# Second-block weights centred by a matmul and split bank by bank inside the first block's attention

## The reference

```
block 0, per batch:  h = film(rmsnorm(x)); Q, K, V = h @ q_w, h @ k_w, h @ v_w  (one head, 128 wide)
                     x = x + softmax(Q K^T / sqrt(128)) V @ proj_w
                     x = x + gelu(film(rmsnorm(x)) @ mlp_w1) @ mlp_w2           (128 -> 512 -> 128)
block 1, per batch:  h = layernorm(x) + shift(cond);  q, k, v = h @ Wqkv.T      (16 heads of 64)
                     q, k = layernorm of each head's 64 values
                     x = x + concat(softmax(q k^T / 8) v) @ Wout.T
experts:             8 experts each take the 128 tokens of highest gate, a gelu MLP each, added back
```

## Time and profile before

| | before |
|---|---|
| median of 3 runs | 473.82 us (473.6 to 474.19) |
| the profiled execution | 473.62 us, its span 471.9 us |
| mean granted TensorE clock | 0.949 |
| PE busy | 419.6 us (89% of the span) |
| DVE / ACT / POOL busy | 303.2 / 299.7 / 186.6 us |
| chain that ended last | PE 72%, DVE 5% |

### The profile page before, as it was taken

The page is one execution under the profiler, slowest core; times in us unless marked ns, Lnnn a source line. Parts: engine busy times, 40 slices in busy tenths (PEclk is TensorE's granted clock), DMA queues, the critical chain, the costliest instruction groups (busy, mean ns, idle before and its releaser), DMA issues.

```text
span 471.9 us, 8986 instructions
## 1 busy us (share of the span) xinstructions
PE 419.6 (89%) x2918; PEld 363.0 (77%) x2918; DVE 303.2 (64%) x761; ACT 299.7 (64%) x675; POOL 186.6 (40%) x148
## 2 busy tenths in 40 slices
PE   2998965389999999999999999999998987639996
PEld 1577554269989999999999998999997886528794
DVE  3574365556776776776777677677676437985233
ACT  3255523357878878878887887887886666305631
POOL 5102472734543553553454454355354004235000
PEclk9999997579999999999999999999999997858999
DMA  8300000650000000000000000000000000000001
GB/s 230 106 1 1 1 0 0 193 209 1 1 3 1 1 1 0 0 0 0 0 0 0 0 0 0 0 0 0 0 0 2 1 0 2 0 2 0 1 1 44
DMA packets 7492, 9.49 MB, mean 20 GB/s; under 512 B 371, under 2 KB 4270, under 8 KB 7470
## 3 DMA queue, kind: packets, MB, share of 16 engines
q1 hardware_dynamic: 5646, 7.11, 4.9%
q10 hardware_dynamic: 1824, 2.10, 1.6%
HBM read 8.68 MB, written 0.52 MB: 20 GB/s over the span
## 4 chain that ended last, share of the span: by engine, by line
PE 72%; DVE 5%; issue 1%; ACT 1%; DVEq 0%
PE bank L1255 24%; PE bank L1040 16%; PE pair L1221 9%; PE pair L1240 6%; PE pair L1239 6%; PE bank L1406 2%; PE pair L1040 1%; PE pair L1327 1%; DVE at_least L941 1%; PE pair L1362 1%; PE bank L1362 1%; PE pair L1398 1%; PE pair L1417 1%; PE pair L1379 1%; PE bank L1398 1%
## 5 line engine op out<-in xcount | busy, mean ns | idle before, releaser
L1255 PE MATMUL bank<-v_s,probs_T 128*128 128x128 f32 x1024 | 135.4, 275 | 2.7 <-ACT probs_T L596 1.9
L857 DVE TENSOR_REDUCE negmax<-pair 128x1 f32<-128x512 f32 x128 | 88.1, 688 | 74.8 <-PE pair L1240 74.8
L1255 PEld LDWEIGHTS bank<-v_s,probs_T 128*128 128x128 f32 x1024 | 126.5, 192 | 5.9 <-issue 2.5
L416 POOL TENSOR_TENSOR qk_rstd<-qk_ms,minus_half 128x8 f32<-128x8 f32 x32 | 55.1, 1721 | 132.2 <-DVE qk_ms L828 132.0
L596 ACT ACTIVATE probs_T<-bank 128x512 f32<-128x512 f32 x128 | 76.6, 598 | 44.6 <-PE bank L1040 44.6
L590 ACT ACTIVATE probs<-pair,negmax 128x512 f32<-128x512 f32 x128 | 88.2, 689 | 15.9 <-DVE negmax L857 15.8
L1040 PE MATMUL bank<-ident,probs 128*128 128x128 f32 x512 | 76.6, 272 | 0.0
L1040 PEld LDWEIGHTS bank<-ident,probs 128*128 128x128 f32 x512 | 62.7, 140 | 13.2
L1239 PE MATMUL pair<-k_s,q_s 128*128 128x512 f32 x128 | 61.4, 480 | 0.4 <-ACT probs L590 0.4
L1240 PE MATMUL pair<-k_low,q_s 128*128 128x512 f32 x128 | 50.8, 397 | 0.0
L426 POOL TENSOR_TENSOR q_s<-kq,k_s 64x512 fp32r<-64x512 f32 x32 | 44.0, 1376 | 13.5 <-DVE k_s L843 8.7
(11 more groups left out here) (260 smaller groups left out, 659.5 us busy)
## 6 DMA issues: line engine op xcount, KB each, us to landing
fc_raw<-in_L_cond_fc2s_dram SPq DMA_DIRECT2D x1, 2048.0 KB, 15.2
x_in<-in_x_dram ACTq DMA_DIRECT2D x1, 512.0 KB, 4.7
w<-in_L_cond_mlp_w_dram SPq DMA_DIRECT2D x2, 256.0 KB, 3.2
wout<-in_L_cond_Wout_dram SPq DMA_DIRECT2D x1, 512.0 KB
b_all<-in_L_cond_b2s_dram SPq DMA_DIRECT2D x1, 512.0 KB, 11.5
out_dram<-final SPq DMA_DIRECT2D x2, 256.0 KB, 2.4
film<-in_L_cond_film_w_dram SPq DMA_DIRECT2D x2, 128.0 KB, 5.1
wq<-in_L_cond_q_w_dram SPq DMA_DIRECT2D x1, 64.0 KB, 7.3
```

The costliest lines, as they stand in the source:

```text
L416: pool.tensor_tensor(qk_rstd[:, :, :].rearrange("p c t -> p (c t)"), qk_ms[:, :, :].rearrange("p c t -> p (c t)"), minus_half[:, 0:2 * NC] ...
L857: dve.tensor_reduce(negmax[:, s:s + 1], bank[s % 2][:, :], AX, ALU.max, negate=True)\
L1255: last = pe.matmul(bank[4][:, c * D:c * D + D], probs_T[:, c % 2, k, :], v_s[:, slot, k, :], start=(k == 0), stop=(k == NC - 1))
```

## The change

- `w_all` and `wmean` go. A constant matrix `centring` (identity minus 1/64 in the two 64x64 diagonal blocks) is built on POOL at the start. The four banks of q and k weights are products raw x `centring` (L1151 of the changed file) where they were transposes: they come out turned and centred.
- Each bank is split at once: ACT rounds it from PSUM into `w_hi`, DVE subtracts, PSUM minus `w_hi`, into `w_lo` (`weights_low`, L768). POOL has no part in it any more.
- The six first banks are made in iterations g = 1 to 6 of block 0's attention, all in PSUM bank 7, so each waits until the one before is copied and split; in DVE's list the subtraction of bank g-2 stands behind the maximum and the scaling of iteration g. Of the other four, one stands before `proj0(1)`, one after, two after the up products of batch 0.
- The MLP goes batch by batch: up products 0 to 3, transposes of batch 1's norm, two weight banks, `down0(0)`, up products 4 to 7, transposes of batch 0's second-block norm, `down0(1)`. POOL adds the MLP bias per batch. ACT writes batch 0's `h_T` in two halves and DVE splits it in two halves.
- `project(3)` moves into the first unit, behind the second chunk's scores, and ACT's and DVE's work on it with it. The first pieces and batch 1's norm are interleaved in another order.

```diff
             turned0(TC - 2)
...
+            act.wait_ge(mid_ready, 1)
+            square(x_mid, 0)
             turned0(TC - 1)
+            act.wait_ge(exp0_done, TC)
+            act.activation(table_call[:, 0:1], minus_half[:, 0:1], ACT.Gelu)
+            copy_weights(QK_BANKS + WOUT_BANKS)
             into_h(1)
+            act.wait_ge(mid_ready, 2)
+            square(x_mid, 1)
+            copy_weights(QK_BANKS + WOUT_BANKS + 1)
...
+            for n in range(HC):
+                gelu0(n)
+            for n in range(QK_BANKS + WOUT_BANKS + 2, W_BANKS):
+                copy_weights(n)
+            act.wait_ge(wT_done, W_BANKS + 1)
+            act.activation(wgate_T[:, :], bank[6][:, 0:E], ACT.Copy).then_inc(wT_copied, 1)
+            for n in range(HC, 2 * HC):
+                gelu0(n)
             act.wait_ge(norm_in, 1)
             square(xn, 0)
...
+            def weights_low(n):
+
+                dve.wait_ge(wT_copied, n + 1)
+                dve.tensor_tensor(weight_part(w_lo, n), weight_psum(n), weight_part(w_hi, n).bitcast(F32),
+                                  ALU.subtract).then_inc(w_split, 1)
+
             for g in range(TC + 1):
...
+                if 2 <= g <= QK_BANKS + 1:
+                    weights_low(g - 2)
...
+            for b in range(B):
+                at = slice(b * NC, b * NC + NC)
+                pool.wait_ge(norm_done, 3 + b)
+                pool.tensor_tensor(x_mid[:, at, :], x_mid[:, at, :],
+                                   mb0[:, :].unsqueeze(1).to_broadcast([P, NC, D]), ALU.add).then_inc(xmb_ready, 1)
...
+        def weight_bank(n):
+
+            return bank[7] if n < QK_BANKS + WOUT_BANKS else bank[5 + n % 2]
...
+            def make_weights(n):
+                dst = weight_bank(n)
+                if n == 0:
+                    pe.wait_ge(wqkv_in, 16)
+                    pe.wait_ge(v0_ready, 1)
+                    pe.wait_ge(centring_ready, 1)
+                elif n <= QK_BANKS + WOUT_BANKS:
+                    pe.wait_ge(wT_copied, n)
+                    pe.wait_ge(w_split, min(n, QK_BANKS))
+                if n < QK_BANKS:
+                    for c in range(4):
+                        last = pe.matmul(dst[:, c * P:c * P + P], wqkv_raw[:, 4 * n + c, :], centring[:, :],
+                                         start=True, stop=True)
...
             for g in range(TC + 3):
...
+                if 1 <= g <= QK_BANKS + WOUT_BANKS:
+                    make_weights(g - 1)
                 if g == NC + 3:
+                    pe.wait_ge(wT_copied, QK_BANKS + WOUT_BANKS)
                     proj0(0)
+            make_weights(QK_BANKS + WOUT_BANKS)
             proj0(1)
...
+            turn_norm(1, 0)
+            pe.wait_ge(mlp_in, 32)
+            pe.wait_ge(h_act, 2)
+            for n in range(HC):
+                up0(n)
+            turn_norm(1, 1)
+            for n in range(QK_BANKS + WOUT_BANKS + 2, W_BANKS):
+                make_weights(n)
+            down0(0)
...
+            for n in range(HC, 2 * HC):
                 up0(n)
+            turn_norm(2, 0)
             down0(1)
-            turn_norm(2, 0)
...
             project(0, 0, 0)
+            pe.wait_ge(h_split, 2)
             project(1, 1, 0)
+            pe.wait_ge(norm_in, 2)
+            turn_piece(0, 0)
             turn_norm(2, 1)
-            turn_piece(0, 0)
             turn_piece(1, 1)
-            pe.wait_ge(h_split, 2)
+            pe.wait_ge(h_split, 3)
             project(2, 2, 0)
-            project(3, 3, 0)
             body(0, first=True)
```

More of the change, by code:

```diff
@@ L543, in _ @@
                                bias=col("mlp_b1", c)).then_inc(gelu0_done, 1)
[L544 to L548 removed]
+            for n in range(HC):
[6 more added lines that the diff above has]
+                gelu0(n)
             act.wait_ge(norm_in, 1)
             square(xn, 0)
[L552 removed]
+            act.wait_ge(norm_T, 5)
+            for half in range(2):
+                act.activation(h_T[:, half * (N // 2):(half + 1) * (N // 2)],
+                               bank[1][:, half * (N // 2):(half + 1) * (N // 2)], ACT.Identity,
+                               bias=affine[:, 2, 1, 0:1], scale=affine[:, 2, 0, 0:1]).then_inc(h_act, 1)
             act.activation(table_call[:, 0:1], minus_half[:, 0:1], ACT.Exp)
[L554 to L556 removed]
             def piece_in(p, p_in):
@@ L601, in body @@
                     u = i * PER + j
+                    start = first and j == 0
                     for c in range(NC):
                         g = u * NC + c
-                        if c == 0 and not (last and j >= PER - 3):
+                        if c == (2 if start else 0) and not (last and j >= PER - 3):
                             piece_in(u + 3, j + 3)
@@ L607, in body @@
                             piece_affine(u + 2)
-                        if not (first and j == 0 and c < 2):
+                        if not (start and c < 2):
                             copy_probs(g - 2, c)
@@ L615, in _ @@
             piece_in(1, 1)
+            act.wait_ge(norm_in, 2)
+            square(xn, 1)
             piece_affine(0)
@@ L812, in _ @@
             sum_squares(2, 0)
-            rest = slice(POOL_HEADS, H)
-            dve.wait_ge(w_centred, 2)
-            dve.tensor_tensor(w_lo[:, rest, :], w_all[:, rest, :], w_hi[:, rest, :].bitcast(F32),
-                              ALU.subtract).then_inc(w_split, 1)
             scaled(2, 0, xn)
+            for half in range(2):
+                dve.wait_ge(h_act, 3 + half)
+                split_h(half * (N // 2), (half + 1) * (N // 2))
             block_out(1)
-            split_h(0)
-            sum_squares(2, 1)
             def piece_ss(p):
@@ L875, in body @@
                     u = i * PER + j
+                    start = first and j == 0
                     for c in range(NC):
                         g = u * NC + c
-                        if c == 3 and not (first and j == 0):
+                        if c == 3 and not start:
                             unit_out(u - 1, (j + 1) % 2, (j + 3) // 2 % 2)
                         chunk_max(g, c)
-                        if c == 0 and not (last and j >= PER - 3):
+                        if c == (2 if start else 0) and not (last and j >= PER - 3):
                             piece_ss(u + 3)
@@ L884, in body @@
                             piece_high(u + 2, j + 2)
-                        if c == 2 and not (last and j >= PER - 3):
+                        if c == (3 if start else 2) and not (last and j >= PER - 3):
                             piece_norm(u + 3, j + 3)
@@ L1264, in body @@
                         scores(g, u, c, j)
+                        if first and j == 0 and c == 1:
+                            project(3, 3, 0)
                         if c == 0 and not (last and j >= PER - 2):
```

191 lines of the change are left out of this document (74 added, 117 removed).

## The result

The changed kernel takes 478.84 us (median of 4 runs, 477.9 to 479.57) against 474.0 for the kernel before on the same chip: ratio 1.0105, 95% interval 1.0089 to 1.0122. The forecast was 478.7. The profiled execution took 478.36 us, its span 476.6, against 473.62 and 471.9 before.

A forecast was written before the change was run, and what follows sets the result against it. Before the loop at 105.33 the kernel was taken as bound in turn by full PE in attention, then PE's waits for DVE, POOL and ACT. Terms -0.2, +3.3 and +1.8 (clock) gave +5.1 on 473.62: 478.7 us; range 474.5 to 483.5.

The forecast's parts named there:

- two of its own signs: Before and in the loop: project(2) starts near 90, project(4) 3 to 5 us later than 103.83.
- Attention: Block 0's attention: chunks take 4.02 us instead of 2.19, banks waiting for DVE's split; ends at 47.25, not 39.90: +7.35.
- rival 2: Block 0's attention: the wait hides and a bank costs only its products; 3.7 us less, 475.0; chance 0.08.
- To the first up product: After block 0's attention: six banks of transposes and copies gone; up product at 52.0, before 46.92; 2.3 us won back.
- Batch 0's MLP: Block 0, up products through batch 0's down products: 62.6, before 61.2, a smaller POOL stall included; 3.6 us won back.
- Batch 0's second norm: After batch 0's last up products: transposes at 70.4, before 71.40, -1.0 in all.
- Down products of batch 1: Behind batch 0's second-norm transposes: first projection at 74.55 instead of 74.71, -0.2; plus +1.8 for half clock.
- Rival 1: Half clock takes all of down0(1), and the later DVE multiply waits for both POOL passes: 480.6 to 482.1; chance 0.23.
- First pieces: Before the loop: project(2) at 90.3, before 86.1, +4.2; piece 2's norm ready at 97.2 instead of 95.5, +1.7.
- Project(3) in the loop: Transposes and scores stand ahead: its first square at 101.8 instead of 98.51, loop start +3.3; this step +1.6.
- rival 4: Project(3) in the loop frees nothing, already in the sum; if PE did get ahead, 1.6 less: 477.1.
- Rival 3: Before the loop: clock stays full from 70 through project(3), making the kernel faster: 472.3 us; chance 0.1.

The follow-up runs named there:

- experiment 1: Changed kernel with the six weight banks of block 0's attention taking PSUM banks 7 and 6 in turn, not 7 alone: 475.38 us.
- experiment 2: Changed kernel with POOL's MLP bias of batch 0 issued ahead of its scale for batch 1's norm: 478.33 us.
- Experiment 5: Changed kernel with four dummy products of 512 columns ahead of the transposes of batch 0's second norm: 477.34 us.
- experiment 4: Changed kernel with project(3), and ACT's and DVE's work on it, back ahead of the unit loop: 478.89 us.
- experiment 8: Changed kernel with two POOL waits, so its subtractions of pieces 0 and 1 start only after DVE's norm multiply and h_lo: 478.6 us.
- experiment 9: Changed kernel with the four dummy products of experiment 5 plus short ones in PE's gaps up to the loop, leaving the one ahead of project(4): 474.97 us.
- 10: The kernel of experiment 7 with short dummy products in its gaps ahead of the loop, nine of them behind the wait they should fill: 470.95 us.
- experiment 12: The kernel of experiment 9 with ten more short dummy products in the wait ahead of project(4): 473.76 us.
- experiment 3: Changed kernel with batch 1's down products put back ahead of the transposes of batch 0's second norm: 476.29 us.
- 6: Changed kernel with the edits of experiments 1, 2 and 3 together: 471.82 us.
- 7: The kernel of experiment 6 with batch 1's second norm and split ahead of the first pieces' own work on ACT, DVE, POOL and PE: 470.04 us.
- 11: The kernel of experiment 10 with the nine dummy products moved ahead of their wait and ten more ahead of project(4): 466.72 us.

## Why the prediction was right

The sum (+5.1) and the time (478.7) hold, but not every term, and two of its own signs didn't come: project(2) near 90 (93.88), and project(4) 3 to 5 us later than 103.83 (5.73). In the old trace's time:

*Attention*, +7.35: measured 39.90 to 47.25, exact. The step behind it, a bank that waits for DVE's split, is shown by experiment 1; rival 2 (the wait hides) is out, since the period is 4.06 and not 3.1.

*To the first up product*, 2.3 won back, and *Batch 0's MLP*, 3.6 won back: up product at 52.02 (forecast 52.0), transposes of batch 1 at 56.33 (56.2). The POOL meeting was there (1.75), and experiment 2 takes it away.

*Batch 0's second norm*: transposes at 70.49 (70.4).

*Down products of batch 1*, with the clock term of +1.8. Rows first: PE ran transposes and down products in 5.48 us at a mean granted clock of 0.71, project(0) came at 75.97 where the full-clock sum had 74.55. Experiment 5 prices the clock at 1.5 us, by traces and by medians. The 1.8 was half of the largest possible, a choice between ends, and that it came near was luck: the price isn't a constant. The same 16 products behind the same gap took 4.82 us in the changed kernel's trace, 4.73 in experiment 2's, 5.82 in 4's, 6.21 in 1's and 4.76 in 8's, against 3.84 at full clock.

Rival 1 was that all of them run at half clock. It didn't come: they would have taken 7.4 us, and the longest was experiment 1's 6.21. The Trainium skill's rule behind it ("TensorE: Matmul & The Clock Gate", the section on PE-mode transpose: transposes don't count as busy for the clock) isn't tested by these runs beyond: in experiment 5 the transposes stood in the same place and with the gap ahead of them filled nothing ran at half clock, so the idle 4.13 us were enough for what was seen.

*First pieces*, forecast from project(0) to project(2) 15.75 us, was 17.91. This step failed, by 2.2 us. Up to batch 1's multiply it held (forecast end 87.2 with the clock term, measured 87.00, meeting with `q_s` included). Behind it two things were missing: the two banks of transposes were given 1.0 us and took 2.0 at half clock (87.05 to 89.02), and `h_lo` was given its plain price inside the 1.15 of the split, but met POOL's `k_low` and took 1.63. The first cause is priced by experiment 9, where the clock was full: from project(0) to project(2) it took 17.15 us. Experiment 8 shows the meeting behind the second, not its worth alone, since it took both meetings away. The prediction had seen one meeting and did not go on to look for the next pass of DVE with two SBUF inputs. It also gave POOL's `q_s` the 1.27 of `k_low`; in that trace `q_s` took 1.51. From project(2) to the transposes of piece 2 the forecast was 6.9, and 6.98 came.

*Project(3) in the loop*, +1.6, failed the other way: +0.42 in the traces, and experiment 4 gets just that back. The step that failed is that project(4) follows piece 3's square with nothing between that could give way. The square came 4.14 us behind the point at which piece 2's norm was ready (100.86 to 105.00), not the 4.6 of the forecast, since the clock was full again for the last two products of project(3). In the kernel before it was 2.96 (95.55 to 98.51). Of these 1.18 more 0.76 came back behind the square, which now reaches project(4) in 4.56 us, not 5.32 (98.51 to 103.83). In the kernel before DVE had stood at the maxima of chunks 0 and 2: the sum began 0.87 us behind the square's end and the norm 0.51 behind POOL's power, and now it is 0.57 and 0.03. The result is near what rival 4 forecast (1.6 less), but by this way, not by PE getting ahead.

*What follows the loop* was taken as unchanged. It is 0.77 us shorter in the trace. The granted clock differs in it: the logits took 1.49 us before at 390.00, and 1.06 after. That is no effect of the change. No experiment changes anything there, and the stretch took 84.60 to 84.76 us in the traces of experiments 2, 5, 10 and 12 (84.75 in the changed kernel's) and 85.43 to 85.57 in those of 1, 3, 4, 6, 7 and 11 (85.52 in the kernel before's); experiments 8 and 9 have 85.28 and 86.69.

So +2.2 (first pieces), -1.2 (project(3)), -0.4 (clock) and -1.0 (the loop and what follows it) against the sum come to -0.4. That the sum is so near is luck, since the last four terms cancel; the terms of attention, MLP and second norm are each within 0.2 us. Rival 3 didn't happen by itself (granted clock 0.72 from project(0) to project(2)), but its mechanism was sound: with the clock kept full the change lost its cost. Its price was too high. The prediction gave it 6.4 us in all (472.3), and experiment 12 shows 5.1 (473.76).

## What to carry to other kernels

When work moves into a loop that was full on one engine, read off how long another engine's queue holds the buffer back, not only what the work costs; a second buffer gave back 3.5 of the 4.8 us. Look through a chain for every DVE pass with two SBUF inputs that a POOL pass can meet, since removing or moving POOL work shifts all meetings behind it. Where TensorE waits for other engines in a latency-bound stretch, its own clock is a cost on that path: put real work into the gap first (experiment 3), dummy products otherwise, and always ahead of the wait. And before a difference of 1 to 2 us between two traces is put down to an edit, look whether the clock fell in a stretch that the edit doesn't touch.

## What the runs showed of the hardware

A 128x512 `tensor_tensor` of DVE with both inputs in SBUF takes 0.69 us alone. With a POOL pass of 1.26 to 1.32 us begun 0.06 to 0.24 us earlier it took 1.63 to 1.75, and it ended 0.55 us after POOL's (93.82 and 93.27), about when a pass would end that had been held until POOL was through. The Trainium skill's page "SBUF — State Buffer", section "Who interferes with whom", says the same: a DVE pass with two SBUF inputs contends with a POOL pass that reads SBUF for a pair of ports that is under "an exclusive lock", and the order of issue decides who waits. The traces agree: in these three meetings POOL had begun first. The other order is in the kernel before: DVE's `w_lo` pass ran from 65.03 to 66.25, and POOL's step begun at 65.21 took 1.10 us where it takes 0.19 elsewhere. A wait that orders the two (experiment 8) restored 0.69 both times.

The price of an idle gap on TensorE varied from execution to execution. Behind the same 4.1 us of waiting, the same 16 down products lost between 0.9 and 2.4 us. Behind the same 2.8 us ahead of project(4), seven traces lost nothing and three lost 1.4 to 1.6. The times of the changed kernel go with the granted clock too: it took 477.9 and 478.36 in the executions with a mean granted clock of 0.953, and 479.32 and 479.57 in those with 0.943. Filling most gaps did not narrow the spread (473.89 to 477.71 in experiment 9), and filling the last one did (472.62 to 474.53 in experiment 12). What else sets the moment at which the clock falls or returns these runs don't show.
